# Four transformer blocks in one program: the second MLP product as three fp32r terms, and twelve score tiles a step ahead where a step has no MLP

## The chip, the cores and the metric

The kernel runs on one core of a Trainium2 chip. The metric is device time in microseconds (us) from the program's first to its last instruction; lower is better. In this text PE is the matrix engine (TensorE), PEld its weight loads, DVE the vector engine (VectorE), ACT the scalar engine (ScalarE), POOL the GpSimd engine, and SP the queue that issues most DMAs (SyncE). A line such as L1179 is a line of the kernel before; where the change is shown, the line numbers are those of the changed file.

## What is computed

Eight sequences of 256 tokens, 256 wide, go through four transformer blocks. Each block normalises, modulates by a vector made from the conditioning input, runs attention with 16 heads of width 16, and adds the result back. Blocks 0, 1 and 3 then do the same with an MLP of width 1024; block 2 has a modulated norm in its place. Block 1's attention is causal. All is float32.

```python
# blocks 0, 1 and 3 (block 1 with a causal mask); sh, sc, gt come from cond @ W_ada + b
h = layernorm(x) * (1 + sc1) + sh1
q, k, v = heads(h @ Wqkv)
x = x + gt1 * (softmax(q @ k.T / sqrt(16)) @ v @ Wo + bo)
h = layernorm(x) * (1 + sc2) + sh2
x = x + gt2 * (gelu(h @ W1 + b1) @ W2 + b2)
# block 2: scores unscaled, out-projection scaled by 1/sqrt(256),
# and after attention: x = x + gamma * layernorm(x) + beta, with no MLP
```

## The kernel before

**Steps.** The program is a chain of 32 steps, one for each pair of block (layer) and sequence: step g is layer g // 8, sequence g % 8. The order of instructions on each engine is written out by hand, and semaphores alone tie the engines together. In step g four sequences are in work: g itself is in the middle of its attention, c = g - 1 finishes (output projection, first residual, second norm, MLP), a = g + 1 gets its queries, keys and values, and n = g + 2 its first norm. A step has MLP work when c's layer has an MLP: steps 1 to 16 and 25 to 31, and sequence 31 after the last step. Steps 17 to 24 have none. The helper names used below: `q_product`, `k_product`, `v_product` (L1110, L1125), `projection` (L1139), `mlp_up` and `mlp_down` (L1165, L1179) on PE; `modulate1`, `query_hi`, `key_hi`, `value_copy`, `exps`, `gelus` on ACT; `query_lo`, `key_lo`, `ln1_a`, `ln1_c` (L777), `max_copy` (L822) on DVE.

**Exact products.** A plain fp32 product of PE runs as two recorded matmuls. The reduced form fp32r runs as one, but on rounded operands. The first MLP product `mlp_up` is therefore made of three fp32r terms: high part times high part, high times low, low times high. POOL makes the high and low parts of W1 once for each layer (`split_w1`, L474 and L476), and DVE those of the activations in each step (`ht2_split`, L908 and L910). The second product `mlp_down` is plain fp32: 16 products of a 128x128 block of `hid` and a 128x256 block of W2.

**Scores and maxima.** Queries and keys are split likewise, stored to DRAM (`spill`) and read back in an interleaved layout (`stack`: six DMAs for `q_stack`, three for `k_stack`), so that scores come from one pass. The 16 heads and two query halves make 16 score tiles of a sequence. `score` computes tile j into one of two PSUM banks and may begin when tile j - 2 has been read; DVE reads it in `maxima` (L805, or L800 where causal) and keeps the maximum of each row. The maxima of eight tiles are then split, transposed on PE (`max_turn`, L1213), copied (`max_copy`) and sent by DMA into two more rows of `q_stack` (`max_rows`, L285). `score_t` computes the scores a second time, transposed and with the maxima taken off (L1240), ACT takes the exponentials (`exps`, L613), and `values` (L1256) multiplies by V, once for heads 0 to 7 and once for 8 to 15. In step g tiles 8 to 15 of g and tiles 0 to 7 of a are made: eight tiles run one step ahead.

**The order around the change.** In an MLP step PE runs `mlp_up`, then tile 0 of a, and then the 16 products of `mlp_down` in small groups between `score_t(g, 4..7)`, tiles 1 to 7 of a and `values(g, 1)`. On POOL, `power` (L444, L446) makes the reciprocal deviations of the two norms: for c early in the step, for n once DVE has its variances. DVE's `ln1_c` waits for the latter and stands before tile 2 of a in DVE's order. In steps 17 to 24 PE begins with tiles 8 and 9, then the q and k products, then `score_t(g, 0)` and tiles 10 to 15 with the rest between them; ACT runs `query_hi` and `key_hi` before any exponential.

## Time and profile before

| what | value |
|---|---|
| median of three runs | 1170.08 us (1169.41 to 1170.24) |
| span of the profiled execution | 1170.3 us |
| PE busy | 1081.3 us, 92% |
| DVE busy | 746.0 us, 64% |
| ACT busy | 569.9 us, 49% |
| POOL busy | 174.5 us, 15% |
| mean granted clock of PE | 0.982 |

Busy time is the union of an engine's recorded instructions. PE's matmuls overlap and their ends are modelled, so how fast a stream of matmuls goes is read from their starts. An entry in brackets at the end of a timeline row is the time in which the engine stood idle before it, and what ended that.

### The profile page before, as it was taken

To read this page: it belongs to the slowest core of one execution; us is meant where nothing else is said; L and a number is where in the kernel's file an instruction comes from. 1 tells how busy PE (TensorE), PEld (TensorE's weight loads), DVE (VectorE), ACT (ScalarE), POOL (GpSimd) and SP (SyncE) were. 2 spreads that over 40 slices of the span, in tenths; PEclk is the share of its full clock that TensorE was granted. 3 is DMA by queue.
4 is the path that set the end of the run, shared out by engine and by line. 5 is a ranking of instruction groups with operands and counts; after the bars stand their busy time and mean duration, and the time that the engine had idled before them with its cause. 6 is when DMAs were issued, how large, how long until landed. Compare 5 with 4: busy or idle time off the path is not lost.

```text
span 1170.3 us, 21598 instructions
## 1 busy us (share of the span) xinstructions
PE 1081.3 (92%) x7618; PEld 858.1 (73%) x7618; DVE 746.0 (64%) x2091; ACT 569.9 (49%) x1140; POOL 174.5 (15%) x288
## 2 busy tenths in 40 slices
PE   5899999999999999999999988888888999999997
PEld 4568878788787787888787755556556877887776
DVE  4476656766567666667665666666667666676632
ACT  4254565554553445544446434444445556555452
POOL 3011110111113111101111101111114111011110
PEclk9799999999999999999999999988999999999999
DMA  7732333222345223331233433323343133321300
GB/s 236 244 115 63 102 110 109 80 65 73 110 155 186 77 78 110 110 110 60 69 102 109 137 111 102 115 94 109 110 152 128 58 100 119 119 89 66 106 4 19
DMA packets 102715, 123.21 MB, mean 105 GB/s; under 512 B 8992, under 2 KB 96032, under 8 KB 101600
## 3 DMA queue, kind: packets, MB, share of 16 engines
q1 hardware_dynamic: 102048, 121.73, 33.4%
q8 instruction: 54, 0.88, 0.3%
q10 hardware_dynamic: 576, 0.30, 0.1%
q14 instruction: 37, 0.30, 0.1%
HBM read 85.16 MB, written 35.78 MB: 103 GB/s over the span
## 4 chain that ended last, share of the span: by engine, by line
PE 71%; DVE 10%; DMA 8%; ACT 5%; issue 3%; SPq 1%; ACTq 1%; POOL 0%; DVEq 0%; POOLq 0%
PE dense L1179 13%; PE o_banks L1256 9%; PE dense L1110 9%; PE dense L1165 9%; PE s_bank L1203 8%; DMA q_stack<-max_t 7%; PE st_bank L1240 6%; PE o_banks L1139 4%; DVE neg_max L805 3%; PE o_banks L1264 3%; PE o_banks L1089 2%; ACT probs L613 2%; PE o_banks L1125 2%; PE s_bank L1213 2%; PE st_bank L1232 1%
## 5 line engine op out<-in xcount | busy, mean ns | idle before, releaser
L613 ACT ACTIVATE probs<-st_bank 128x512 f32<-128x512 f32 (+1 forms) x512 | 264.5, 570 | 172.9 <-PE st_bank L1240 121.7
L805 DVE TENSOR_REDUCE neg_max<-s_bank 128x2 f32<-128x512 f32 x384 | 256.7, 685 | 120.9 <-PE s_bank L1203 117.5
L1203 PE MATMUL s_bank<-k_stack,q_stack 96*128 96x256 f32 (+1 forms) x1024 | 233.9, 319 | 19.2 <-DMA k_stack<-qk_dram 10.1
L1203 PEld LDWEIGHTS s_bank<-k_stack,q_stack 96*128 96x128 f32 x1024 | 169.9, 194 | 61.7 <-DVE neg_max L805 20.2
L1179 PE MATMUL dense<-w_sb,hid 128*128 128x256 f32 x768 | 204.9, 381 | 0.0
L1240 PE MATMUL st_bank<-q_stack,k_stack 98*128 98x512 f32 x384 | 152.8, 471 | 15.6 <-DMA q_stack<-max_t 12.5
L444 POOL TENSOR_TENSOR veps<-mv,eps_c 128x2 f32<-128x2 f32 x65 | 13.7, 210 | 901.7 <-DVE mv L771 901.7
L1179 PEld LDWEIGHTS dense<-w_sb,hid 128*128 128x128 f32 x768 | 128.8, 189 | 9.6 <-issue 0.4
L601 ACT ACTIVATE hid<-dense,vec 128x256 f32<-128x256 f32 x192 | 80.6, 471 | 110.8 <-PE dense L1165 110.7
L1256 PE MATMUL o_banks<-probs,v_aug 128*32 128x256 f32 (+1 forms) x2048 | 124.9, 387 | 9.9 <-DVE xg L844 5.8
L1110 PE MATMUL dense<-ht,w_sb 128*128 128x256 f32 x512 | 127.2, 388 | 3.9 <-ACT ht L555 1.3
L1165 PE MATMUL dense<-ht,w_hi 128*128 128x256 f32 x384 | 116.4, 303 | 7.7 <-DVE ht_lo L910 6.5
L800 DVE CUSTOM_DVE_ANT_0 s_bank<-s_bank,mask_q 128x128 f32<-128x128 f32 (+1 forms) x256 | 86.3, 382 | 53.4 <-PE s_bank L1203 52.9
L1110 PEld LDWEIGHTS dense<-ht,w_sb 128*128 128x128 f32 x512 | 95.8, 194 | 18.0 <-issue 5.7
L1165 PE MATMUL dense<-ht_lo,w_hi 128*128 128x256 f32 x384 | 108.3, 282 | 0.0
L1165 PE MATMUL dense<-ht,w_lo 128*128 128x256 f32 x384 | 108.3, 282 | 0.0
L1256 PEld LDWEIGHTS o_banks<-probs,v_aug 128*32 128x32 f32 x2048 | 64.6, 114 | 56.2 <-issue 18.4
L1240 PEld LDWEIGHTS st_bank<-q_stack,k_stack 98*128 98x128 f32 x384 | 67.8, 190 | 44.7 <-ACT probs L613 17.5
L1165 PEld LDWEIGHTS dense<-ht,w_hi 128*128 128x128 f32 x384 | 72.9, 190 | 19.7 <-DVE ht_lo L910 10.4
L877 DVE COPY o_sb<-o_banks 128x512 f32<-128x512 f32 x46 | 31.8, 692 | 69.9 <-PE o_banks L1256 69.9
L1165 PEld LDWEIGHTS dense<-ht_lo,w_hi 128*128 128x128 f32 x384 | 73.2, 191 | 0.0
L1165 PEld LDWEIGHTS dense<-ht,w_lo 128*128 128x128 f32 x384 | 73.0, 190 | 0.0
(126 smaller groups left out, 1447.5 us busy)
## 6 DMA issues: line engine op xcount, KB each, us to landing
q_stack<-qk_dram SPq DMA_DIRECT2D x192, 128.0 KB, 2.9
k_stack<-qk_dram SPq DMA_DIRECT2D x96, 256.0 KB, 4.0
par_sb<-par_dram SPq DMA_DIRECT2D x32, 512.0 KB, 5.2
qk_dram<-q_hi SPq DMA_DIRECT2D x32, 256.0 KB, 2.1
qk_dram<-q_lo SPq DMA_DIRECT2D x32, 256.0 KB, 2.2
qk_dram<-k_hi SPq DMA_DIRECT2D x32, 256.0 KB, 2.1
qk_dram<-k_lo SPq DMA_DIRECT2D x32, 256.0 KB, 2.1
w_sb<-w SPq DMA_DIRECT2D x3, 1280.0 KB, 7.5
```

Source lines behind the costliest of these rows:

```text
L601: ins = nc.scalar.activation(hid[:, 2 * i + k], src[:, k], ACT.Gelu, bias=col(l, "b1", 2 * i + k))
L613: nc.scalar.activation(probs[p % 4][:, kt, :, q0:N], src, ACT.Exp, scale=SCORE_SCALE[l]).then_inc(p_sb, 1)
L800: ins = nc.vector.tensor_tensor_reduce(out=s, in0=s, in1=mask_q[:, (1 - qt) * P:2 * P], scale=-1.0, scalar=-MASKED, op0=ALU.add, op1=ALU.m ...
L805: nc.vector.tensor_reduce(neg_max[:, qt, 2 * p:2 * p + 2], split3(bank[:]), AX.X, ALU.max, negate=True).then_inc(s_max, 1)
L1110: ins = mm(dense[bank][:, t * N:(t + 1) * N], w_qkv(a.layer, kt, c0, c0 + P), ht1[:, kt], start=kt == 0, stop=kt == KT - 1)
L1139: ins = mm(o_bank[0][:, t * D:(t + 1) * D], ao_t[:, kt, t * P:(t + 1) * P], w_o(c.layer, kt), start=kt == 0, stop=kt == KT - 1)
L1165: ins = mm(dense[(i + 1) % 2][:, k * N:(k + 1) * N], w, h.bitcast(F32R), start=n == 0, stop=n == len(terms) - 1)
L1179: ins = mm(dense[1][:, t * D:(t + 1) * D], hid[:, j, t * P:(t + 1) * P], w_2(c.layer, j), start=j == 0, stop=j == FT - 1)
L1203: ins = mm(bank[:, e * N:e * N + k1], q_stack[g.par][0:KB, 2 * p + e, qt * P:(qt + 1) * P].bitcast(F32R), k_stack[g.par][0:KB, p, 0:k1].bi ...
L1240: mm(split3(st_bank[kt][:]), *stacks(g, p, kt, 0), start=True, stop=True).then_inc(st_ps, 1)
L1256: ins = mm(o_bank[i][32 * j:32 * j + 32, q0:N], v_aug[g.par][:, kt, 8 * h + 4 * i + j, :], pr[:, kt, j % 2, q0:N], start=kt == 0, stop=kt ...
L1264: ins = tr(o_bank[i][:, N + t * P:N + (t + 1) * P], o_sb[:, i, t * P:(t + 1) * P], ident[:])
```

## The change

It has two parts.

**The second product.** `mlp_down` becomes 48 fp32r matmuls in place of 16 fp32 ones: each product of a `hid` block and a W2 block is `hid_hi` x `w2_hi`, `hid_hi` x `w2_lo`, `hid_lo` x `w2_hi`. DVE makes `hid_hi` in four casts of 128x512 (`hidden_hi`), POOL makes `hid_lo` in four subtractions of 128x512 (`hidden_lo`), both in every MLP step. POOL splits W2 once a layer (`split_w2`, in steps 0, 9 and 25). The split of W1 moves ahead of the second norm's `power` in step 9, and from step 25 to step 24. The weights share memory in a new way: W1 of layer 1 is loaded behind the modulation weights, `q_hi` to `k_lo` lie where `hid` is, so the first GELU also waits for the spills of a; W1 has a semaphore of its own, W2 of layer 3 is loaded a step earlier, and the modulation weights of layer 3 two steps later.

**The steps without MLP work.** Steps 17 to 24 get an order of their own on PE, DVE and ACT (`attention_step`), and SP sends both halves of the maxima. Sequences 18 to 24 have twelve of their tiles made one step ahead in place of eight, so that four are left for the beginning of their own step, ahead of `q_product`.

```diff
+        w2_lo = [sb_at(f"w2_lo{i}", [P, FT, D], w_at[i] + O_2 * 4) for i in range(2)]
+        w2_hi = [sb_at(f"w2_hi{i}", [P, FT, D], w_at[1 - i] + O_1 * 4) for i in range(2)]
...
+        hid_at = xn2_at + T * D * 4
+        hid = sb("hid", [P, FT, N])
+        hid_lo = sb_at("hid_lo", [P, FT, N], hid_at)
+        hid_hi = sb("hid_hi", [P, FT, N])
+        q_hi, q_lo, k_hi, k_lo = (
+            sb_at(n, [P, KT, N], hid_at + i * KT * N * 4) for i, n in enumerate(("q_hi", "q_lo", "k_hi", "k_lo")))
...
+        def early_tiles(g):
+            return 3 * H // 4 if g.reg is None and 2 * B + 1 < g.off <= 3 * B else H // 2
...
+                if c.exists and not mlp:
+                    max_rows(sp, g, 1)
...
-                if a.exists and HAS_MLP[g.layer]:
+                if a.exists:
...
-                    load_weights(l + 1, O_O, O_2 if HAS_MLP[l + 1] else O_1, w_ld)
+                    load_weights(l + 1, O_O, O_1, w_ld)
+                    if HAS_MLP[l + 1]:
+                        load_w1(l + 1)
+                    if l + 1 == 3:
+                        load_weights(3, O_2, WCOLS, w2_ld)
...
+            def split_w2(l):
+                pool.wait_ge(w2_ld[l], 16)
+                for i in range(FT // 2):
+                    raw = w_sb[l % 2][:, O_2 + 2 * i * D:O_2 + 2 * (i + 1) * D].rearrange("p (j d) -> p j d", j=2)
+                    hi, lo = w2_hi[l % 2][:, 2 * i:2 * i + 2], w2_lo[l % 2][:, 2 * i:2 * i + 2]
+                    nc.gpsimd.tensor_copy(hi.bitcast(F32R), raw).then_inc(w2_hi_sb, 1)
+                    pool.wait_ge(w2_hi_sb, mlps_before(l) // B * FT // 2 + i + 1)
+                    nc.gpsimd.tensor_tensor(lo.bitcast(F32R), raw, hi, ALU.subtract).then_inc(w2_split, 1)
...
+            def hidden_lo(c, *chunks):
+                for i in chunks:
+                    wait(pool, hid_hi_sb, c.mlp(4, i + 1))
+                    js = slice(2 * i, 2 * i + 2)
+                    nc.gpsimd.tensor_tensor(hid_lo[:, js].bitcast(F32R), hid[:, js], hid_hi[:, js],
+                                            ALU.subtract).then_inc(hid_lo_sb, 1)
...
+                mlp = c.exists and HAS_MLP[c.layer]
                 if g.reg is None and g.off == 0:
                     split_w1(0)
+                if g.reg is None and g.off in (B + 1, 3 * B):
+                    split_w1(g.layer)
                 if c.exists:
                     power(c, 1, ln2_mv, ln2_veps, ln2_rstd)
                     if c.layer != 2:
                         pick(c, 1, mod2_now)
-                    if g.reg is None and g.off % B == 1 and g.layer > 0 and HAS_MLP[g.layer]:
-                        split_w1(g.layer)
+                if g.reg is None and g.off in (B + 1, 3 * B + 1):
+                    split_w2(g.layer)
+                if mlp:
+                    hidden_lo(c, 0, 1, 2)
                 if n.exists:
                     power(n, 0, ln1_mv, ln1_veps, ln1_rstd)
+                if mlp:
+                    hidden_lo(c, 3)
+                if n.exists:
                     wait(pool, xn1_done, n.count(1, 1))
...
-            def gelus(c):
+            def gelus(c, a):
                 l = c.layer
                 for i in range(FT // 2):
                     if i == 0:
                         wait(act, w2_ps, c.mlp(1, 0))
+                        if a.exists:
+                            wait(act, q_spill, a.count(32, 32))
+                            wait(act, k_spill, a.count(32, 32))
                     wait(act, w1_ps, c.mlp(4, i + 1))
...
+            def attention_step(g):
+                c, a = g.back(1), g.ahead(1)
+                modulate1(a)
+                if c.off > 2 * B:
+                    ao_transposed(c)
+                exps(g, 0)
+                query_hi(a)
+                exps(g, 1)
+                key_hi(a)
+                exps(g, 2, 3)
+                value_copy(a)
+                out_copy(g, 0)
+                exps(g, 4, 5, 6, 7)
+                out_copy(g, 1)
+                if g.layer > 2:
+                    ao_transposed(g)
...
+            def hidden_hi(c, *chunks):
+                for i in chunks:
+                    wait(dve, gelu_sb, c.mlp(4, i + 1))
+                    js = slice(2 * i, 2 * i + 2)
+                    nc.vector.tensor_copy(hid_hi[:, js].bitcast(F32R), hid[:, js]).then_inc(hid_hi_sb, 1)
...
+            def attention_step(g):
+                c, a, n = g.back(1), g.ahead(1), g.ahead(2)
+                modulated = modulation_of(g)
+                first, early = early_tiles(g), early_tiles(a)
+                maxima(g, *range(first, H))
+                max_split(g, 1)
+                max_copy(g, 1)
+                query_lo(a)
+                key_lo(a)
+                first_residual(c)
+                wait(dve, x1_done, c.count(1, 1))
+                norm_stats(x1, 1, ln2_stats)
+                wait(dve, ln2_stats, c.count(1, 1))
+                norm_mv(1, ln2_mv)
+                second_norm(c)
+                ln1_a(n)
+                wait(dve, ln1_stats, n.count(1, 1))
+                norm_mv(0, ln1_mv)
+                out_norm(g, 0)
+                ln1_c(n)
+                maxima(a, 0, 1, 2)
+                second_residual(c)
+                maxima(a, 3, 4, 5, 6, 7)
+                max_split(a, 0)
+                if modulated:
+                    modulation_cols(modulated)
+                out_norm(g, 1)
+                max_copy(a, 0)
+                maxima(a, *range(H // 2, early))
+                if modulated:
+                    modulation_rows(modulated)
             def step(g):
...
+                    hidden_hi(c, 0, 1)
                     if n.exists:
                         ln1_a(n)
                         wait(dve, ln1_stats, n.count(1, 1))
+                    hidden_hi(c, 2)
...
+                    hidden_hi(c, 3)
...
             def mlp_down(c, lo, hi):
+                l = c.layer
                 for i in range(lo, hi):
                     t, j = i // FT, i % FT
                     if i == 0:
-                        pe.wait_ge(w2_ld[c.layer], 16)
                         wait(pe, gelu_sb, c.mlp(4, 3))
-                    if i == 6:
-                        wait(pe, gelu_sb, c.mlp(4, 4))
-                    ins = mm(dense[1][:, t * D:(t + 1) * D], hid[:, j, t * P:(t + 1) * P], w_2(c.layer, j),
-                             start=j == 0, stop=j == FT - 1)
+                    if t == 0 and j % 2 == 0:
+                        pe.wait_ge(w2_split, (mlps_before(l) // B) * FT // 2 + j // 2 + 1)
+                        wait(pe, hid_lo_sb, c.mlp(4, j // 2 + 1))
+                    terms = ((hid_hi, w2_hi), (hid_hi, w2_lo), (hid_lo, w2_hi))
+                    for n, (h, w) in enumerate(terms):
+                        ins = mm(dense[1][:, t * D:(t + 1) * D], h[:, j, t * P:(t + 1) * P].bitcast(F32R),
+                                 w[l % 2][:, j].bitcast(F32R), start=j == 0 and n == 0,
+                                 stop=j == FT - 1 and n == len(terms) - 1)
                     if i == T * FT - 1:
                         ins.then_inc(w2_ps, 1)
...
+            def attention_step(g):
+                c, a, n = g.back(1), g.ahead(1), g.ahead(2)
+                modulated = modulation_of(g)
+                first, early = early_tiles(g), early_tiles(a)
+                def modulation_part(part):
+                    if modulated:
+                        modulation_cols(modulated, part=part, parts=4)
+                score(g, *range(first, H))
+                q_product(a, 0)
+                max_turn(g, 1)
+                q_product(a, 1)
+                score_t(g, 0)
+                k_product(a)
+                score_t(g, 1)
+                v_product(a, 0)
+                score_t(g, 2)
+                v_product(a, 1)
+                score_t(g, 3)
+                projection(c, 0)
+                projection(c, 1)
+                if modulated:
+                    wait(pe, q_lo_sb, a.count(1, 1))
+                modulation_part(0)
+                values(g, 0)
+                modulation_part(1)
+                score_t(g, 4)
+                out_turn(g, 0)
+                score_t(g, 5)
+                score(a, 0, 1)
+                score_t(g, 6)
+                score(a, 2)
+                modulation_part(2)
+                score_t(g, 7)
+                score(a, 3, 4)
+                modulation_part(3)
+                values(g, 1)
+                score(a, 5, 6)
+                out_turn(g, 1)
+                score(a, 7)
+                max_turn(a, 0)
+                score(a, *range(H // 2, early - 1))
+                ht1_t(n)
+                ao_turn(g)
+                score(a, *range(max(H // 2, early - 1), early))
+                if modulated:
+                    modulation_rows(modulated)
```

How the order stands now is shown at three places, first on PE in a step without MLP, around the beginning of the step (L1203 and L1340 score tiles, two matmuls each; L1213 and L1350 the transposed maxima; L1110 and L1243 q and k products; L1240 and L1377 `score_t`). Before:

```order
L1213 MATMUL s_bank<-ident,max_parts 16x128 x2
L1203 MATMUL s_bank<-k_stack,q_stack 128x256 x4
L1110 MATMUL dense<-ht,w_sb 128x256 x8
L1240 MATMUL st_bank<-q_stack,k_stack 128x512 x2
L1203 MATMUL s_bank<-k_stack,q_stack 128x256 x4
L1125 MATMUL o_banks<-w_sb,ht 128x256 x2
L1240 MATMUL st_bank<-q_stack,k_stack 128x512 x2
```

And now:

```order
L1350 MATMUL s_bank<-ident,max_parts 16x128 x2
L1340 MATMUL s_bank<-k_stack,q_stack 128x256 x6
L1222 MATMUL o_banks<-ident,xn 128x128 x4
L1222 MATMUL o_banks<-ident,ao 128x128 x4
L1340 MATMUL s_bank<-k_stack,q_stack 128x256 x10
L1243 MATMUL dense<-ht,w_sb 128x256 x2
L1350 MATMUL s_bank<-ident,max_parts 16x128 x2
L1243 MATMUL dense<-ht,w_sb 128x256 x2
L1377 MATMUL st_bank<-q_stack,k_stack 128x512 x2
L1243 MATMUL dense<-ht,w_sb 128x256 x4
L1377 MATMUL st_bank<-q_stack,k_stack 128x512 x2
```

Tiles 8 to 15 now stand in a row before the first q product, where two tiles stood, and no tile stands between it and `score_t(g, 5)`.

Second, ACT at the same place, from the end of one step into the next (L555 and L619 `modulate1`; L584 and L648 `ao_transposed`; L285 the DMA of the maxima; L529 and L593 `query_hi` and `key_hi`; L613 and L680 exponentials). Before:

```order
L571 ACTIVATE o_sb<-o_banks 128x512
L584 ACTIVATE ao_t<-o_banks,bv_scaled 128x256 x2
L555 ACTIVATE ht<-o_banks,mod_now 128x256 x2
L285 DMA q_stack<-max_t 1x8x256 x2
L529 ACTIVATE q_hi<-dense,vec 128x256 x2
L529 ACTIVATE k_hi<-dense,vec 128x256 x2
L613 ACTIVATE probs<-st_bank 128x512 x8
```

And now:

```order
L635 ACTIVATE o_sb<-o_banks 128x512
L619 ACTIVATE ht<-o_banks,mod_now 128x256 x2
L648 ACTIVATE ao_t<-o_banks,bv_scaled 128x256 x2
L680 ACTIVATE probs<-st_bank 128x512 x2
L593 ACTIVATE q_hi<-dense,vec 128x256 x2
L680 ACTIVATE probs<-st_bank 128x512 x2
L593 ACTIVATE k_hi<-dense,vec 128x256 x2
L680 ACTIVATE probs<-st_bank 128x512 x4
```

The high parts of queries and keys each stand behind a pair of exponentials.

Third, POOL in an MLP step (L462 and L499 the pick of a modulation; L444 with L446, and L481 with L483, `power`; L455 and L492 the addends of the residuals). Before:

```order
L462 COPY mod_now<-mod 128x4
L444 TENSOR_TENSOR veps<-mv,eps_c 128x2
L446 TENSOR_TENSOR rstd<-veps,half_c 128x2
L455 TENSOR_TENSOR xg<-xg,par_sb 128x512
L455 TENSOR_TENSOR xg<-x_sb,par_sb 128x512
```

And now:

```order
L499 COPY mod_now<-mod 128x4
L529 TENSOR_TENSOR hid_lo<-hid,hid_hi 128x512 x3
L481 TENSOR_TENSOR veps<-mv,eps_c 128x2
L483 TENSOR_TENSOR rstd<-veps,half_c 128x2
L529 TENSOR_TENSOR hid_lo<-hid,hid_hi 128x512
L492 TENSOR_TENSOR xg<-xg,par_sb 128x512
L492 TENSOR_TENSOR xg<-x_sb,par_sb 128x512
```

Three subtractions stand ahead of the `power` of n, and one between it and the addends.

## Rows read from the trace of the kernel before

**Rows 1.** The page: engines' busy time, and the chain that ended last.

```profile
PE 1081.3 (92%) x7618; PEld 858.1 (73%) x7618; DVE 746.0 (64%) x2091; ACT 569.9 (49%) x1140; POOL 174.5 (15%) x288
PE 71%; DVE 10%; DMA 8%; ACT 5%; issue 3%; SPq 1%; ACTq 1%; POOL 0%; DVEq 0%; POOLq 0%
```

**Rows 2.** Busy time by stretch: bounds, length, engines in the order of the page, clock, DMA.

```profile
198.00:233.00 35.00, 34.91 (x250) 28.66 (x250) 23.50 (x55) 19.55 (x40) 4.62 (x8) 1.00 0.31 92
764.00:795.00 31.00, 26.92 (x165) 18.53 (x164) 19.63 (x48) 13.51 (x27) 4.47 (x7) 0.89 0.32 103
833.55:862.61 29.06, 24.10 (x165) 17.18 (x165) 19.78 (x48) 13.69 (x27) 4.51 (x7) 1.00 0.50 155
```

**Rows 3.** Timeline after the last step (start, us, engine, line): both MLP products.

```profile
1152.43 0.28 PE L1165 MATMUL dense<-ht_lo,w_hi 128*128 128x256 f32 x1
...
1153.97 0.28 PE L1165 MATMUL dense<-ht,w_lo 128*128 128x256 f32 x1
...
1159.14 7.07 PE L1179 MATMUL dense<-w_sb,hid 128*128 128x256 f32 x32
1159.34 0.84 ACT L601 ACTIVATE hid<-dense,vec 128x256 f32<-128x256 f32 x2 [0.60 <-PE dense L1165]
```

**Rows 4.** Timeline of step 4 (layer 0), from the second GELU to tile 4.

```profile
199.78 0.84 ACT L601 ACTIVATE hid<-dense,vec 128x256 f32<-128x256 f32 x2 [1.27 <-PE dense L1165]
200.09 0.41 DVE L822 COPY max_t<-s_bank 16x256 f32<-16x256 f32 x1
...
201.43 0.84 ACT L601 ACTIVATE hid<-dense,vec 128x256 f32<-128x256 f32 x2 [0.81 <-PE dense L1165]
...
202.87 0.84 ACT L601 ACTIVATE hid<-dense,vec 128x256 f32<-128x256 f32 x2 [0.60 <-PE dense L1165]
...
204.31 0.69 POOL L446 TENSOR_TENSOR rstd<-veps,half_c 128x2 f32<-128x2 f32 x1
...
205.28 0.73 DVE L777 TENSOR_SCALAR xn<-x_sb,mv,rstd 128x256 f32 x2
...
208.15 0.40 PE L1203 MATMUL s_bank<-k_stack,q_stack 96*128 96x256 f32 x2
```

**Rows 5.** Lines L908, L777 and L476: durations in ns, min/median/max.

```profile
L908 DVE CAST ht<-xn x24: 426/427/891, 84.0 to 1151.0; 128x512 fp32r<-128x512 f32 x24
...
L777 DVE TENSOR_SCALAR xn<-xg,mv,rstd x48: 402/410/1433, 80.8 to 1148.7; 128x256 f32<-128x256 f32 x48
...
L476 POOL TENSOR_TENSOR w_lo<-w_sb,w_hi x12: 1262/1272/1330, 22.6 to 904.4; 128x512 fp32r<-128x512 f32 x12
```

**Rows 6.** Timeline of step 7 (causal tiles): maxima copied, and tile 4.

```profile
304.98 0.41 DVE L822 COPY max_t<-s_bank 16x256 f32<-16x256 f32 x1
...
314.22 0.34 PE L1203 MATMUL s_bank<-k_stack,q_stack 96*128 96x128 f32 x2
```

**Rows 7.** Timeline of step 23 (no MLP), q product to the next one.

```profile
833.55 3.69 PE L1110 MATMUL dense<-ht,w_sb 128*128 128x256 f32 x16
...
838.72 0.98 PE L1240 MATMUL st_bank<-q_stack,k_stack 98*128 98x512 f32 x2
839.07 2.56 DVE L805 TENSOR_REDUCE neg_max<-s_bank 128x2 f32<-128x512 f32 x4
839.18 0.36 SPq L331 DMA_DIRECT2D qk_dram<-k_lo  x1
839.32 1.08 ACT L613 ACTIVATE probs<-st_bank 128x512 f32<-128x512 f32 x2 [0.17 <-PE st_bank L1240]
...
843.47 1.91 SPq L348 DMA_DIRECT2D k_stack<-qk_dram  x3
...
850.39 0.72 PE L1203 MATMUL s_bank<-k_stack,q_stack 96*128 96x256 f32 x4
```

**Rows 8.** Issues by DMA in 820 to 865 us: KB each, median us to landing.

```profile
k_stack<-qk_dram SPq DMA_DIRECT2D x3, 256.0 KB, 4.2
```

**Rows 9.** Timeline of step 9: `power` of the second norm, before the split of W1.

```profile
367.92 0.20 POOL L444 TENSOR_TENSOR veps<-mv,eps_c 128x2 f32<-128x2 f32 x1 [18.35 <-DVE mv L771]
```

## What the change is expected to do

> **What bounds the kernel now.** I read the page first. PE is busy 92% of the span and makes up 71% of the chain that ended last, DVE 10%, DMA 8% [rows 1]. That is a mean over two kinds of step, so I took one window of each. In an MLP step PE has work in 34.91 of 35.00 us while DVE has 23.50 and POOL 4.62; such a step is bound by PE. A step without MLP has 24.10 of 29.06 us on PE and 19.78 on DVE: nobody is full, and the step is as long as its waits make it [rows 2]. So work taken off PE should pay in full in the MLP steps, unless something new makes PE wait, and a new order in the other steps must be judged by its chain, not by its work. The profiled span, 1170.3, and the median, 1170.08, are as good as one number; I sum against the span.
>
> **Part 1, what it takes off PE.** After the last step both products run with little between them. The 32 records of the fp32 product take 7.07 us from first start to last end; less the drain of the last (0.38) that is 0.216 us each, 0.432 us for a product of two. In the fp32r stream 13 steps from start to start take 1153.97 - 1152.43 = 1.54 us, so 0.1185 each and 0.355 for three terms [rows 3]. One product saves 0.077 us, an MLP 1.2 us, 24 MLPs 29 us. That is the most this part can give. Had the three terms gone no faster than the two fp32 records, the gain would be nil; nothing in the rows suggests it, since `mlp_up` already has this shape.
>
> **Part 1, what it adds.** Four casts on DVE (0.43 us each, L908 is the same form) and four subtractions on POOL (1.27 each, L476 is the same form) [rows 5]. DVE has 11 us to spare in the window and POOL 30. But products 0 and 1 now need the first cast and subtraction, products 6 and 7 the fourth, and the `power` of n stands behind three subtractions. I lay them into step 4 by its rows [rows 4]. The second to fourth GELU end at 200.62, 202.27 and 203.71; DVE is free for the first cast when `max_copy` ends, at 200.50. Two casts follow each other until 201.4.
>
> DVE's casts and POOL's subtractions also hinder each other, as the split of W1 shows: the cast L908 takes 427 ns as a rule and up to 891, the normalisation L777 410 and up to 1433, while L476 on POOL stays between 1262 and 1330 [rows 5]. I therefore let one of the two run at a time where their operands are in SBUF. Then: subtraction 1 from 201.4 to 202.65; cast 3 behind it to 203.1; subtraction 2 to 204.35; cast 4 to 204.8; subtraction 3 to 206.05; `power` (0.2 and 0.7 us) to 207.05; subtraction 4 to 208.35. In the kernel before the deviation was there at 205.00 [rows 4].
>
> The Trainium skill states the same as an exclusive lock on a shared port pair held for the whole instruction (SBUF — State Buffer, the part on engine contention). By that a cast that comes just too late takes 1.27 + 0.43 = 1.70 us, where the longest in the trace is 0.89; with every cast and normalisation at that worst the sum would be some 1 us more for each MLP step. I go by the rows.
>
> What waits: `ln1_c` (L777) began at 205.28; POOL goes on to subtraction 4 at once, so I put it behind that, 208.35 to 209.1. Tile 2 of a is reduced right after it, to 209.8, and PE's tile 4, which needs tile 2 read, starts at 209.85 in place of 208.15 [rows 4]. Products 0 to 6 have saved 0.5 us by then, all of it lost in this wait, with 1.7 us more; the nine products behind give 0.7 back. Step 4 becomes 1.0 us longer. The products 6 and 7 wait for subtraction 4 in the same stretch, which adds nothing. In layer 3 the stretch before tile 4 is about half a microsecond longer already, since `score_t(g, 4)` waits for the maxima there; I take 0.8 as the mean of the 14 steps with non-causal tiles ahead (1 to 6, 15, 16, 25 to 30). In the causal ones (7 to 14) the same layout from `max_copy` at 304.98 brings tile 4 to 314.65 where it was at 314.22 [rows 6]: the tiles start later in them, for a wait on the stacks, and the gap is smaller. With 0.7 given back behind it that is -0.2 us. Sum: 14 x 0.8 - 8 x 0.2 = +9.6. After the last step the fourth GELU ends at 1160.18 [rows 3]; casts and subtractions in turn (1.7 us a chunk, from the first GELU on) end at 1163.2, products 6 to 15 take 3.6 us, and with the drain of the last the end is at 1167.0 in place of 1166.2: +0.8. If POOL and DVE did not hinder each other, `power` would be done at 205.8, tile 4 would start at 207.95, and such a step would win 0.9 us: that is the other bound.
>
> **Part 1, the edges.** Two casts and subtractions for a quarter of W2 take 4 x (0.61 + 1.27 + 0.08) = 7.9 us a layer on POOL. In step 9 the split of W1 stands ahead of `power`; it can begin when layer 0's last product is done (some 361.5), so it ends at 369.4 where `power` began at 367.92 [rows 9]: +1.5. In step 0 the split of W2 holds the pick for `modulate1` until about when ACT needs it: +0.5. The new GELU wait on the spills has long been met. Edges: +2.
>
> **Part 2, the first half of a step.** Zero is the start of the q product; the old step has it at 833.55 [rows 7]. Old: `k_lo` is ready for its spill at 5.63 (839.18), the last of three `k_stack` DMAs is issued at 843.47 + 1.27, at 11.2, and lands 4.2 us on [rows 8], at 15.4. Tile 0 of a is issued at 16.84 and did not wait for it. New: half a q product (0.86); `max_turn` waits until 1.6, for tiles 14 and 15 at 0.64 each [rows 7] and the split; the other half to 2.6; `score_t` 0 to 3.05; k product (8 records) to 4.8; then `score_t` 1, because ACT has an exponential pair in front of `key_hi`. Its first exponential comes 0.60 after its start (838.72 to 839.32) and the pair takes 1.08 [rows 7]: 6.5. `key_hi` to 7.35, `key_lo` and the spill at 8.3, which is 2.65 later than now. SP's nine DMAs behind it are the same: landed at 18.05. PE itself would be there at 15.5 (its wait for the maxima ahead of `score_t` 4 is gone, those for the first residual and for ACT's exponentials stay). So the stacks, which cost nothing now, become the last to arrive, and tile 0 waits 2.5 us.
>
> **Part 2, the second half.** Old: 850.39 to 862.61, 12.2 us, with ten tiles. New: sixteen tiles, and DVE reads one in 0.64 to 0.66, with `second_residual`, a split, `out_norm` and `max_copy` between, of the same lengths as now: tile 4 is issued 2.7 after tile 0, `values(g, 1)` at 3.6, tile 7 at 6.75, `max_turn` 8.45, tile 9 at 9.6 behind `max_copy`, tile 11 at 11.5, tiles 13, 14 and 15 each behind DVE, the next q product at 14.3. A step takes 18.05 + 14.3 = 32.4 us against 29.06. Over steps 17 to 24: first halves 8 x 1.2 = +9.7; seven second halves 7 x 2.1 = +14.7; step 17, which has eight tiles to do ahead of its q product in place of two, +4.7; step 24, which makes only eight early, -1.5. Sum +27.6. Were the stacks in time (15.5 in place of 18.05), it would be 20.4 less, +7.2: that is the lower bound.
>
> **Sum.** 1170.3 + 9.6 + 0.8 + 2 + 27.6 = 1210.3.
>
> **Rivals.** B: engines hinder each other less, or DVE wins the race for `ln1_c`, and MLP steps win 0.9 us (22 of them and the end: -20.3), part 2 as worked out: 1179.6. For it: L908's median is undisturbed. Against: the long casts are those that met the split of W1.
>
> C: MLP steps as worked out, but the stacks come in time, by `key_hi` or the DMAs being faster than I laid them: 1170.3 + 10.4 + 2 + 7.2 = 1189.9.
>
> D, the other side: both, so that PE's saving reaches the span: 1170.3 - 20.3 + 2 + 7.2 = 1159. It holds if `power` of n is done within about 0.6 us of where it was, from where tile 4 no longer waits, and if tile 0 of a waits for no stack. Since part 2 alone is never below +7 by my chain, faster needs both, or a first half of under 14.6 us.
>
> E: more idle time on PE brings its clock down. Steps 20 and 21 show it: a window of 31.00 us has a granted clock of 0.89, the one of 29.06 us has 1.00 [rows 2], with the same instructions. If all eight steps pay these 1.9 us, it is 1210 + 15 = 1225. The Trainium skill has it that idleness sends TensorE back to the lower of its two levels (TensorE: Matmul & The Clock Gate, the part on what is happening), and the trace agrees in that the clock is 1.00 in the fullest window.
>
> **Chances and range.** A (1210) 0.42, B 0.15, C 0.15, D 0.15, E 0.13. The range leaves out D and most of what lies beyond E: 1168 to 1228. Two tenths of a percent, 2.3 us, is about what a measurement can tell from no change. Faster by more: D and a little of B and C, 0.18; within it 0.03; slower 0.79.
>
> **What would show it.** Right: in MLP steps PE waits at tile 4 of a for DVE, the casts of `hid_hi` have a mean well above 0.43 us, L777's successor a mean well above 0.41, and the second product is some 5.7 us of starts. In steps 18 to 23 tile 0 waits about 2.5 us for `k_stack`, and the step takes 32 us. Wrong: no such wait, or steps of 29 us; then the order of ACT was not what decided. If PE's stream of products does not go at 0.12 us a term, the first line of the sum falls.

## The result: 1220.7 us, 4.2% slower

| | before | after |
|---|---|---|
| median of four runs | 1170.16 us (1169.41 to 1173.03) | 1220.71 us (1218.59 to 1224.57) |
| profiled span | 1170.3 us | 1222.8 us |
| mean granted clock of PE | 0.982 | 0.941 |

The ratio is 1.0424, with a 95% interval of 1.0379 to 1.0469. The profiled execution is the slowest of the four, so the two traces lie 52.5 us apart where the medians lie 50.5. The page of the kernel after, its busy times and its chain by engine, against [rows 1]:

```profile
PE 1107.2 (91%) x8002; PEld 897.4 (73%) x8002; DVE 840.0 (69%) x2187; ACT 567.2 (46%) x1140; POOL 328.1 (27%) x408
...
PE 57%; DVE 13%; DMA 8%; issue 7%; SPq 6%; ACT 4%; POOL 3%; DVEq 0%; POOLq 0%; ACTq 0%
```

PE is busy for 26 us more although its second MLP product got cheaper, and its share of the chain fell from 71% to 57%. The first place to look is where the time sits. I took the start of each step's q product in both traces. Steps 0 to 16 together are 2.9 us longer, steps 17 to 24 are 51.6 us longer, the rest is 2 us shorter. So nearly all of the loss is in the steps without MLP work. The windows of the kernel after (length, then busy PE, PEld, DVE, ACT and POOL, then the granted clock), one MLP step, two single steps and all of steps 17 to 24, against [rows 2]:

```profile
221.90:257.20 35.30, 34.80 (x267) 29.02 (x266) 27.26 (x59) 19.52 (x39) 9.96 (x12) 1.00 0.29 90
694.80:734.60 39.80, 31.88 (x166) 22.56 (x165) 20.77 (x48) 13.37 (x27) 5.09 (x7) 0.73 0.27 81
808.00:842.30 34.30, 27.16 (x167) 18.78 (x166) 21.01 (x48) 13.37 (x27) 5.10 (x7) 0.90 0.30 94
...
651.16:947.60 296.44, 241.96 (x1352) 170.78 (x1351) 165.78 (x383) 107.05 (x216) 46.99 (x64) 0.82 0.30 95
```

Before, the same eight steps:

```profile
648.34:893.16 244.82, 208.66 (x1362) 147.09 (x1363) 160.67 (x388) 109.70 (x216) 37.22 (x56) 0.96 0.37 114
```

These two rows split the 51.6 us. PE's idle time rose from 36.2 to 54.5 us, +18.3. Its busy time rose by 33.3 us on the same number of matmuls, with the granted clock down from 0.96 to 0.82. The clock alone accounts for it: 208.7 us of work at 0.96 would be 244 at 0.82 (an estimate from the two rows), and 242 is there.

Step 21 of the kernel after, on PE, SP and ACT, where [rows 7] has step 23 before. The q product starts at 808.02; L1243 is the q and k products, L1377 `score_t`, L1340 a score tile, L1350 `max_turn`:

```profile
809.45 0.39 PE L1350 MATMUL s_bank<-ident,max_parts 128*16 128x128 f32 x2 [0.41 <-DVE max_parts L904]
...
822.21 0.98 PE L1377 MATMUL st_bank<-q_stack,k_stack 98*128 98x512 f32 x2
826.42 1.22 PE L1340 MATMUL s_bank<-k_stack,q_stack 96*128 96x256 f32 x4 [3.22 <-DMA k_stack<-qk_dram]
...
836.64 0.39 PE L1350 MATMUL s_bank<-ident,max_parts 128*16 128x128 f32 x2 [1.27 <-DVE max_parts L904]
...
840.65 1.10 PE L1340 MATMUL s_bank<-k_stack,q_stack 96*128 96x256 f32 x4 [0.55 <-DVE neg_max L892]
...
842.28 1.03 PE L1243 MATMUL dense<-ht,w_sb 128*128 128x256 f32 x4
...
810.32 1.30 SPq L307 DMA_DIRECT2D q_stack<-max_t  x2
812.88 0.37 SPq L357 DMA_DIRECT2D qk_dram<-q_hi  x1
...
816.00 0.36 SPq L357 DMA_DIRECT2D qk_dram<-k_lo  x1
...
820.29 2.79 SPq L374 DMA_DIRECT2D k_stack<-qk_dram  x3
...
813.18 1.09 ACT L680 ACTIVATE probs<-st_bank 128x512 f32<-128x512 f32 x2 [0.32 <-PE st_bank L1377]
814.15 0.84 ACT L593 ACTIVATE k_hi<-dense,vec 128x256 fp32r<-128x256 f32 x2
```

The cast of k comes behind an exponential pair, k_lo is spilled 8.0 us after the start of the q product (5.6 before), and tile 0 of a comes at +18.4, after waiting 3.2 us for the K stack (`k_stack`). That is the picture of the prediction. From tile 0 to the next q product it takes 15.9 us.

### The profile page after: what moved, and what is told of

It reads as the page before. It is cut to its first block, busy times and chain, and to the rows that moved or that the text cites. A ratio compares the mean times of both kernels' runs of the same rounds, so it can differ in the third digit from the quotient of the medians.

```text
span 1222.8 us, 22726 instructions
## 1 busy us (share of the span) xinstructions
PE 1107.2 (91%) x8002; PEld 897.4 (73%) x8002; DVE 840.0 (69%) x2187; ACT 567.2 (46%) x1140; POOL 328.1 (27%) x408
## 4 chain that ended last, share of the span: by engine, by line
PE 57%; DVE 13%; DMA 8%; issue 7%; SPq 6%; ACT 4%; POOL 3%; DVEq 0%; POOLq 0%; ACTq 0%
PE s_bank L1340 8%; PE o_banks L1393 8%; PE dense L1315 8%; PE dense L1243 8%; PE dense L1298 6%; PE st_bank L1377 5%; DMA k_stack<-qk_dram 4%; DVE neg_max L892 4%; SPq L371 4%; PE o_banks L1272 4%; DMA q_stack<-max_t 3%; PE o_banks L1222 3%; POOL hid_lo L529 2%; SPq L374 1%; PE s_bank L1350 1%
## 5 line engine op out<-in xcount | busy, mean ns | idle before, releaser
L680 ACT ACTIVATE probs<-st_bank 128x512 f32<-128x512 f32 (+1 forms) x512 | 264.6, 571 | 216.8 <-PE st_bank L1377 162.5
L1340 PE MATMUL s_bank<-k_stack,q_stack 96*128 96x256 f32 (+1 forms) x1024 | 241.5, 332 | 50.7 <-DMA k_stack<-qk_dram 35.6
L1340 PEld LDWEIGHTS s_bank<-k_stack,q_stack 96*128 96x128 f32 x1024 | 180.3, 211 | 94.1 <-DMA k_stack<-qk_dram 39.8
L529 POOL TENSOR_TENSOR hid_lo<-hid,hid_hi 128x512 fp32r<-128x512 f32 x96 | 125.8, 1320 | 267.2 <-DVE hid_hi L1004 267.2
L1377 PE MATMUL st_bank<-q_stack,k_stack 98*128 98x512 f32 x384 | 157.9, 483 | 6.6 <-DMA q_stack<-max_t 5.9
L481 POOL TENSOR_TENSOR veps<-mv,eps_c 128x2 f32<-128x2 f32 x65 | 17.9, 276 | 518.6 <-DVE mv L858 518.6
L1243 PE MATMUL dense<-ht,w_sb 128*128 128x256 f32 x512 | 135.8, 402 | 1.3 <-ACT ht L619 1.3
L1393 PE MATMUL o_banks<-probs,v_aug 128*32 128x256 f32 (+1 forms) x2048 | 131.0, 401 | 6.5 <-issue 5.8
L1315 PE MATMUL dense<-w_hi,hid_hi 128*128 128x256 f32 x384 | 115.5, 301 | 4.7 <-POOL hid_lo L529 4.6
L1243 PEld LDWEIGHTS dense<-ht,w_sb 128*128 128x128 f32 x512 | 100.0, 204 | 15.5 <-issue 1.7
L1315 PE MATMUL dense<-w_lo,hid_hi 128*128 128x256 f32 x384 | 108.8, 283 | 0.0
L1315 PE MATMUL dense<-w_hi,hid_lo 128*128 128x256 f32 x384 | 108.3, 282 | 0.0
L1377 PEld LDWEIGHTS st_bank<-q_stack,k_stack 98*128 98x128 f32 x384 | 71.3, 201 | 35.8 <-ACT probs L680 19.0
L887 DVE CUSTOM_DVE_ANT_0 s_bank<-s_bank,mask_q 128x128 f32<-128x128 f32 (+1 forms) x256 | 85.6, 383 | 16.1 <-PE s_bank L1340 15.3
L1298 PEld LDWEIGHTS dense<-ht,w_hi 128*128 128x128 f32 x384 | 72.9, 190 | 19.8 <-DVE ht_lo L997 10.5
L1004 DVE CAST hid_hi<-hid 128x512 fp32r<-128x512 f32 x96 | 73.8, 787 | 19.2 <-ACT hid L668 19.1
```

Source lines behind the costliest of these rows:

```text
L529: nc.gpsimd.tensor_tensor(hid_lo[:, js].bitcast(F32R), hid[:, js], hid_hi[:, js], ALU.subtract).then_inc(hid_lo_sb, 1)
L680: nc.scalar.activation(probs[p % 4][:, kt, :, q0:N], src, ACT.Exp, scale=SCORE_SCALE[l]).then_inc(p_sb, 1)
L887: ins = nc.vector.tensor_tensor_reduce(out=s, in0=s, in1=mask_q[:, (1 - qt) * P:2 * P], scale=-1.0, scalar=-MASKED, op0=ALU.add, op1=ALU.m ...
L1004: nc.vector.tensor_copy(hid_hi[:, js].bitcast(F32R), hid[:, js]).then_inc(hid_hi_sb, 1)
L1243: ins = mm(dense[bank][:, t * N:(t + 1) * N], w_qkv(a.layer, kt, c0, c0 + P), ht1[:, kt], start=kt == 0, stop=kt == KT - 1)
L1298: ins = mm(dense[(i + 1) % 2][:, k * N:(k + 1) * N], w, h.bitcast(F32R), start=n == 0, stop=n == len(terms) - 1)
```

## The experiments

The runs below were made together with new runs of the kernel before, which lay between 1166 and 1185 us there; so each is given as a ratio to it, with its 95% interval. The row of the kernel after keeps the ratio of its own measurement. To read the steps without MLP I cut each at tile 0 of a: the **first stretch** runs from the q product to it, the **second stretch** from it to the next q product. Means of steps 18 to 24, each from one trace, and the granted clock over steps 17 to 24:

| kernel | first | second | step | clock | ratio |
|---|---|---|---|---|---|
| before | 16.6 | 13.4 | 30.0 | 0.96 | 1 |
| after | 19.1 | 17.0 | 36.1 | 0.82 | 1.0424 |
| casts ahead | 17.8 | 16.0 | 33.7 | 0.90 | 1.0321 |
| wait filled | 19.3 | 15.4 | 34.7 | 0.89 | 1.0404 |
| eight tiles | 20.0 | 18.1 | 38.2 | 0.78 | 1.0563 |
| product first | 25.1 | 13.8 | 38.9 | 0.81 | 1.0716 |
| tiles beside | 26.4 | 15.5 | 41.9 | 0.77 | 1.0762 |

**Each part alone.** Part 1 alone takes the early return into `attention_step` away on three engines, and SP's part of it:

```diff
-            return 3 * H // 4 if g.reg is None and 2 * B + 1 < g.off <= 3 * B else H // 2
+            return H // 2
-                if c.exists and not HAS_MLP[c.layer]:
-                    attention_step(g)
-                    return
```

> Part 1 alone: the second MLP product as three fp32r terms, with the order and the eight early tiles of the kernel before in the steps without MLP work. In the trace of the changed kernel steps 0 to 16 together took only 2.9 us more than before, and steps 25 to 31 1.9 us less, so the theory that the parts are independent gives 1170.2 + 1.0 = 1171 us (1168 to 1174). The prediction's terms for the MLP work (+9.6, +0.8 and +2) give 1182.6. If the two parts hinder each other (buffers that start at one address, another semaphore for the maxima), part 1 alone is well below before: each step's second product starts and ends 1.2 us earlier, 24 x 1.2 = 29 us, 1141.

Measured 0.9973 (0.9940 to 1.0006): no difference that can be told, as the traces of the two kernels had it. Part 2 alone is the kernel before with `attention_step`, `early_tiles` and SP's order.

> Part 2 alone: the kernel before with the new order of the eight steps 17 to 24, twelve early tiles, and the maxima's rows issued by SP. If the parts are independent the whole loss of steps 17 to 24 is here: 1170.2 + 51.5 = 1222 us (1216 to 1227). By the prediction's terms for part 2 it is 1197.8. If the loss needs part 1 (a clock that is lower because of more fp32r work before), it is under 1190.

Measured 1.0525 (1.0458 to 1.0592). The whole loss is in part 2. It is even larger than in the full change, whose interval just touches this one, and above my 1222. Its trace puts 7.1 us more than the full change into the same eight steps (303.5 against 296.4, at a clock of 0.81); whether part 1 takes that off, or the executions differ, I leave open.

**Casts ahead.** ACT's casts and PE's k product again ahead of the exponentials and of `score_t`, as in the kernel before; the rest of the change kept:

```diff
-                exps(g, 0)
                 query_hi(a)
-                exps(g, 1)
                 key_hi(a)
-                exps(g, 2, 3)
+                exps(g, 0, 1, 2, 3)
...
                 q_product(a, 1)
-                score_t(g, 0)
                 k_product(a)
+                score_t(g, 0)
```

> The changed kernel with the products and casts of Q and K taken ahead again in the eight steps: TensorE makes the K product straight behind the Q product, ahead of the first pair of transposed scores, and ScalarE casts query and key ahead of its exponentials, as the kernel before did. Theory A (the stacks of the next step are asked for too late, since ScalarE casts between exponentials): the wait of the first early score tile for the K stack (3.2 us in step 21, 22.8 us over seven steps) falls under 1 us each, SP's spill of k_lo starts some 3 us sooner behind the Q product, and the time falls by 20 to 25 us for the wait alone, to 1195 to 1200. Rival (the order of VectorE sets the steps: it is the neg_max of each tile that is late): the wait for the stack goes over to a wait for neg_max, and the time stays within 5 us of 1220.7. Rival (the clock): the waits go but the granted clock stays near 0.8, and busy time of TensorE stays at 212 us over the eight steps against 183 before.

Measured 1.0321 (1.0279 to 1.0364), some 12 us less than the change, by two ratios of different measurements whose intervals lie 0.15% apart. PE's longest waits over steps 17 to 24 in the kernel after (total us, times, longest):

```profile
PE s_bank L1340 <- DMA k_stack<-qk_dram: 26.1, 8, 4.7
PE s_bank L1350 <- DVE max_parts L904: 12.2, 13, 1.3
```

and in this one:

```profile
PE s_bank L1348 <- DVE max_parts L902: 12.6, 14, 1.3
PE s_bank L1338 <- DMA k_stack<-qk_dram: 8.9, 7, 2.0
PE st_bank L1375 <- ACT probs L680: 8.1, 8, 1.0
```

The mechanism holds, two thirds of the stack wait went, but half of that came back as a wait for exponentials, which now stand behind the casts. The step is still 3.7 us above the kernel before, 2.6 of it in the second stretch, whose order this edit doesn't touch. By the ratios the late casts are a quarter of the loss; in the traces steps 17 to 24 get 22.2 of their 51.6 us back. The 29.4 us that are left there are read from this trace and not tried: PE is idle for 12.2 us more than in the kernel before, with 12.6 us for the split maxima of a turn where the kernel before waits 3.3, and busy for 17.2 us more, at a clock of 0.90 in place of 0.96.

**The wait filled.** In the seven steps without modulation, 28 matmuls that nobody reads stand in the wait:

```diff
+                if not modulated:
+                    wait(pe, q_lo_sb, a.count(1, 1))
+                    for _ in range(28):
+                        mm(dense[0][:, 0:2 * P], ident_b[:], mask_k[:], start=True, stop=True)
                 score(a, 0, 1)
```

> The changed kernel with 28 matmuls whose results nobody reads (128 x 256, bf16) put ahead of the first early score tile in seven of the eight steps, where TensorE waits for the K stack. Over steps 17 to 24 the changed kernel needs 46.6 us more than before, of which 29.7 are TensorE busy for longer on the same 1190 matmuls (granted clock 0.82 against 0.95) and 16.9 are waits. Theory (the clock falls because TensorE stands still there): the granted clock of the steps rises to 0.95 or more and the time falls to 1190 to 1205. Rival (the clock has to do with other waits or with what came before): the clock stays near 0.82, and the time stays at 1221 or rises by up to 2 us a step, to 1235.

Measured 1.0404 (1.0362 to 1.0446), not to be told from the change. The trace tells more than the ratio. Steps 17 to 24 in its windows:

```profile
655.80:943.42 287.62, 248.77 (x1548) 179.33 (x1547) 167.23 (x383) 107.06 (x216) 45.81 (x64) 0.89 0.32 98
```

and the wait for the stack in them:

```profile
PE s_bank L1340 <- DMA k_stack<-qk_dram: 5.6, 5, 2.5
```

Most of the stack wait is filled (26.1 us to 5.6) and the clock rises from 0.82 to 0.89, so standing still there does lower it. Steps 18 to 24 are 1.4 us shorter on average, all of it in the second stretch (17.0 to 15.4). The first stretch, which ends when the stack lands, is no shorter (19.1 and 19.3). Steps 17 to 24 together are 8.8 us shorter and the whole trace is 5.0 shorter; a gain of that size is at the edge of what the ratio can show. So the clock is a cost on top of the waits: half of its fall was worth 1.4 us a step in this one trace, where my rival E had 1.9.

**Eight tiles.** `early_tiles` returns 8 again, in the full change.

> The changed kernel with eight instead of twelve early score tiles in the eight steps 17 to 24; all else of both parts stays. Theory of the loop (a period is the time from the Q product to the landed stacks, 18.4 us in step 21, and behind it, in a row, sixteen score tiles with their maxima, since the Q product of the next step stands behind the last of the tiles whatever their split; 15.9 us): the time stays, 1214 to 1228, and tile 0 still waits 2 to 5 us for the K stack. Rival (the four tiles that were taken ahead lengthen the step on VectorE, four times 0.65 us each step): 2.6 us x 7 = 18 us less, 1202.

Measured 1.0563 (1.0490 to 1.0636): both expectations were wrong. Twelve early tiles are better than eight in this order. Comparing step 21 of the change with step 22 of this run: from `max_turn(a, 0)` to the next q product it is 5.6 us with twelve tiles and 7.7 with eight. With twelve, the two groups of transposes at the step's end lie between tiles, beside DVE's maxima; with eight nothing is left to do beside them. This is argued from rows, not tried.

**Product first.** With the casts ahead, PE's q and k products also ahead of tiles 12 to 15, and DVE's subtractions ahead of their maxima.

```diff
-                score(g, *range(first, H))
                 q_product(a, 0)
-                max_turn(g, 1)
                 q_product(a, 1)
+                k_product(a)
+                score(g, *range(first, H))
+                max_turn(g, 1)
```

> The changed kernel with the casts ahead (as in the run before it) and, in the eight steps, TensorE's Q and K products also ahead of the last score tiles 12 to 15 and the turn of the maxima, VectorE's subtractions ahead of those tiles' maxima. Theory of the loop: the remaining tiles (about 4 x 0.9 us) then lie beside the way of the stacks and not ahead of it, and the steps fall from 33.8 us to 30 to 31 us, 8 x 3 = 24 us below the 1211.3 measured with the casts ahead: 1185 to 1192. Rival (VectorE or the maxima's rows set the steps): the transposed score tile 4 waits longer for the maxima's rows instead and the time stays at 1205 to 1215.

Measured 1.0716 (1.0636 to 1.0796). The second stretch did what the theory of the loop said, 16.0 to 13.8. The first grew from 17.8 to 25.1. SP's timeline (q product at 815.84) has a part of the reason:

```profile
826.69 1.30 SPq L307 DMA_DIRECT2D q_stack<-max_t  x2
828.04 0.44 SPq L357 DMA_DIRECT2D qk_dram<-q_hi  x1
...
829.57 0.50 SPq L357 DMA_DIRECT2D qk_dram<-k_lo  x1
```

The maxima's rows of g stand ahead of the spill in SP's order, and SP waits for them: `q_hi` is cast by 819.9 and spilled 8 us later. I had moved work on PE and DVE and not looked at the queue behind which the spill stands. But PE is late as well:

```profile
820.33 0.83 PE L1338 MATMUL s_bank<-k_stack,q_stack 96*128 96x256 f32 x4
823.25 1.10 PE L1338 MATMUL s_bank<-k_stack,q_stack 96*128 96x256 f32 x4 [2.09 <-DVE neg_max L890]
825.62 0.60 PE L1348 MATMUL s_bank<-ident,max_parts 128*16 128x128 f32 x2 [1.27 <-DVE max_parts L902]
...
841.88 1.09 PE L1338 MATMUL s_bank<-k_stack,q_stack 96*128 96x256 f32 x4 [2.29 <-DMA k_stack<-qk_dram]
```

It is ready for tile 0 at 839.6, already 23.8 us behind the q product, and then waits 2.3 us for the stack; over steps 17 to 24 that wait is 10.9 us, hardly more than the 8.9 with the casts ahead. The larger part of the growth is tiles 12 to 15 and their turn, which now stand in the first stretch with their waits (5.5 us from 820.33), and the lower clock (0.81 against 0.90).

**Tiles beside.** Twelve early tiles with the kernel before's order of the first half: tiles 12 to 15 between `score_t(g, 0)` and `score_t(g, 2)`. It uses the later terms and split of part 1 described below.

> The better part 1 with a part 2 mended by the readings so far: twelve early tiles stay, but the last tiles 12 to 15 stand behind the Q and K products, between the transposed scores, as in the kernel before (first pair of transposed scores ahead of them), with casts and subtractions of Q and K ahead. In the changed kernel a step is the time from Q product to the first early tile (19.1 us) and from there over all sixteen tiles to the next Q product (17.0 us); in the kernel before it is 16.6 + 13.4 with ten tiles in the second stretch. Theory of the loop: the first stretch is the stacks' own 17.5 us, the second has twelve tiles, 14 to 14.7 us: steps of 31.5 to 32.2 us, 7 x 2 us above part 1's 1164, 1174 to 1181, far below 1220. Rival (it is the twelve early tiles as such, on VectorE and on SP's queue): steps stay at 34 to 36 us, 1195 to 1210. Second rival (with the tiles beside the stacks the early ones are pure gain): below 1164.

Measured 1.0762 (1.0676 to 1.0848). Here SP's order is the reason (q product at 821.28; the last row is from the waits of steps 17 to 24):

```profile
832.81 1.30 SPq L307 DMA_DIRECT2D q_stack<-max_t  x2
834.15 0.44 SPq L357 DMA_DIRECT2D qk_dram<-q_hi  x1
...
847.52 1.22 PE L1343 MATMUL s_bank<-k_stack,q_stack 96*128 96x256 f32 x4 [8.91 <-DMA k_stack<-qk_dram]
...
PE s_bank L1343 <- DMA k_stack<-qk_dram: 74.2, 8, 10.8
```

PE is ready for tile 0 at 838.6, 17.3 us behind the q product, and the stack comes 8.9 us later. In the kernel before, ACT sent these rows in such steps, and SP spilled `q_hi` at +2.9. In the change they are SP's, ahead of the spill; this fits `max_turn` standing inside the q product there, with all sixteen tiles in a row. Whether twelve tiles pay with the rows on another queue stayed untried.

**Where part 1's saving goes.** First the terms with `hid_lo` two chunks of j later in the first half of `mlp_down`, on top of part 1 alone:

```diff
-                    terms = ((hid_hi, w2_hi), (hid_hi, w2_lo), (hid_lo, w2_hi))
+            for j in range(FT + 2):
+                if j < FT:
+                    DOWN += [(j, 0, w2_hi), (j, 0, w2_lo)]
+                if j >= 2:
+                    DOWN.append((j - 2, 1, w2_hi))
```

> Part 1 alone, with the terms of hid_lo taken two chunks of j later in the first half of the second product (the products with hid_hi run ahead). In an MLP step of part 1 alone TensorE waits 0.49 us at the first term with hid_lo and 0.46 us at the one of the last chunk, while the step is 35.2 us as before. Theory (TensorE's waits for POOL's hid_lo eat the saving): 0.5 to 0.9 us a step less in the 22 MLP steps, 1148 to 1157 where part 1 alone measured 0.9973 of before (1167). Rival (something else sets the step: the maxima's rows for the transposed score tile 4, or VectorE with its four casts): within 4 us of 1167.

Measured 0.9976 (0.9943 to 1.0010). PE's waits for `hid_lo` are gone from the trace (1.7 us in steps 1 to 16 without the edit) and steps 1 to 7 still take 35.16 us on average, against 35.20 in part 1 alone and 35.65 before, where one step of 37.6 raises the mean. Then POOL's split of layer 0's W2 in step 1 in place of step 0:

> The kernel with the later hid_lo terms, and POOL's split of the first layer's W2 moved from the end of step 0 into step 1, behind the copy of the scale and shift that step 1's Q product waits for. In part 1 alone step 0 is 41.2 us against 36.6 before, with that copy 8.5 us later on POOL. Theory (the copy behind the split costs the 4.6 us, and they are not given back): 4 to 5 us below the run with the later terms. Rival (what step 0 loses is given back later, or step 1 now waits for w2_split): within 1.5 us of it.

Measured 0.9949 (0.9913 to 0.9985). POOL copies the scale and shift for step 1's q product at 66.75, where part 1 alone has:

```profile
75.57 0.18 POOL L497 COPY mod_now<-mod 128x4 f32<-128x4 f32 x1
```

Step 0 falls from 41.2 to 38.2 us, and step 1 takes 2 us of it back (35.2 to 37.3). The fall is no clean measure of the split: PE's idle time in step 0 went from 4.5 to 3.9 us only, the rest is busy time at a clock of 0.84 in place of 0.78, and the run without table loads below, which has the same late split, takes 40.7 us at 0.78. The ratio is 0.3% lower with intervals that overlap. Among the versions that keep every part of the product it is the only one whose interval lies below the kernel before, by 0.5% in the middle.

Next, VectorE's casts in the first MLP step alone. Later steps then take their high part from that old one: `hid_lo` makes up the difference, with coarser rounding.

> Part 1 with the later hid_lo terms and the later split, and VectorE's four casts of hid_hi made in the first step with MLP work only: the later steps multiply with the hid_hi of that step (the product is then not the reference's). It frees VectorE of 3.2 us a step, the drawn-out casts of 1.5 us beside POOL among them. Every MLP step there takes 35.1 to 35.3 us whether transposed tile 4 comes 18.7 or 20.4 us behind the Q product. Theory (ScalarE is the floor: last Gelu, table load of 1.28 us, exponentials 4 to 7): the steps stay at 35.0 to 35.2, within 3 us of 1164 (0.9949 of before). Rival (VectorE's maxima of the early tiles behind the casts are the floor, neg_max waits of 0.45 us at tile 3): 0.5 to 0.9 us a step less, 1145 to 1153.

Measured 0.9922 (0.9885 to 0.9960). Then ACT's table loads away, in part 1 and in the kernel before:

> Part 1 with the later hid_lo terms and the later split, and the Gelu replaced by the identity, with both table loads of an MLP step left out (the product is then not the reference's). Theory (ScalarE's way from the last Gelu over the table load to the exponentials 4 to 7 is the floor under the step): the MLP steps fall from 35.2 to about 34.0 to 34.3 us, the whole by 20 to 25 us against 1164, to 1140 to 1145, and this kernel is 15 to 25 us below its twin without the three-term product. Rival (the floor is VectorE, or the maxima's rows): under 5 us less than 1164.

> The kernel before with the same edit: Gelu replaced by the identity, no table loads (the product is then not the reference's). If TensorE itself sets the MLP steps of the kernel before (34.98 of 35.20 us busy in step 5), nothing is won: 1165 to 1171, steps of 35.0 to 35.2. If ScalarE's way is the floor there too, it falls by 10 to 25 us as well, and part 1 then still wins nothing against it.

Measured 0.9924 (0.9881 to 0.9968) and 0.9970 (0.9931 to 1.0010). The run without casts fits ScalarE as the floor, but the one without table loads refutes it: no floor was lifted by 1 us. In none of the three does an MLP step that is non-causal throughout (1 to 6, 25 to 29) go below 34.9 us. Their timelines say why. With the casts gone, PE waits at the turn of the maxima:

```profile
234.85 1.28 POOL L528 TENSOR_TENSOR hid_lo<-hid,hid_hi 128x512 fp32r<-128x512 f32 x1 [9.11 <-ACT hid L665]
234.97 1.19 DVE L896 CAST max_parts<-neg_max 128x16 fp32r<-128x16 f32 x1
...
236.50 0.38 PE L1350 MATMUL s_bank<-ident,max_parts 128*16 128x128 f32 x2 [0.50 <-DVE max_parts L898]
```

This run doesn't relieve VectorE cleanly: POOL no longer waits for the casts, its first subtraction falls beside VectorE's split of the maxima, and that small cast takes 1.19 us in place of 0.17.

With the table loads gone, it waits at tile 3 of a, for DVE and its casts:

```profile
247.86 0.50 PE L1334 MATMUL s_bank<-k_stack,q_stack 96*128 96x256 f32 x2 [0.86 <-DVE neg_max L883]
```

Cut at `score_t(g, 4)`, the rest of an MLP step takes 16.0 to 16.4 us in the kernel before whenever it comes. In the kernel after it takes 15.3 to 15.4 when `score_t(g, 4)` comes 19.8 us behind the q product or later (steps 2, 26 to 29), 15.7 at 19.4 (step 4) and 16.4 to 16.5 when it comes by 18.8 (steps 3, 5, 6), with step 1 between (19.0, 16.2); step 25 alone doesn't fit (20.9, 16.3), and has W2's split in it. Step 1 is the same (20.9, 16.4) in the run that moves the split there. PE's own saving of 0.8 us is there, but only in steps where PE comes late to `score_t(g, 4)`. When PE is early it meets ScalarE and VectorE, which are no earlier than before. As I read it, two or three chains end within a few tenths of each other, and taking one away shows the next; taking two away at once wasn't tried. The clock takes a part as well: step 9 has a granted clock of 0.92 to 0.96 in all eleven traces with part 1, and 1.00 in the three without.

## Why the prediction came out as it did

**Direction and range** held: slower, 1220.7 in 1168 to 1228. The point, 1210, missed by 10.7 us. Against the trace (1222.8) it missed by 12.5, through errors that partly cancel: -15.4 for the MLP steps, +5.4 for the edges, +24.0 for part 2 and -1.5 for the end, where I had +0.8. That the point came so close is luck.

**Part 1's price for PE** held: each of the three terms takes 0.12 us from start to start, 0.36 in all, against 0.43 for an fp32 product of two records.

**MLP steps, +9.6: too high.** Steps 1 to 7, 9 to 16 and 25 to 29 came out 5.8 us shorter together. The step that failed is the layout of VectorE and POOL, and with it the wait of PE at tile 4. In step 4 I had tile 4 of a 7.2 us behind tile 0; it came after 5.9 (5.5 before):

```profile
202.30 0.74 DVE L1004 CAST hid_hi<-hid 128x512 fp32r<-128x512 f32 x2
...
204.26 1.47 DVE L1004 CAST hid_hi<-hid 128x512 fp32r<-128x512 f32 x1 [0.56 <-ACT hid L668]
...
208.30 1.61 DVE L864 TENSOR_SCALAR xn<-x_sb,mv,rstd 128x256 f32 x2 [0.33 <-POOL rstd L483]
...
202.78 2.66 POOL L529 TENSOR_TENSOR hid_lo<-hid,hid_hi 128x512 fp32r<-128x512 f32 x2 [11.53 <-DVE hid_hi L1004]
...
208.15 1.28 POOL L529 TENSOR_TENSOR hid_lo<-hid,hid_hi 128x512 fp32r<-128x512 f32 x1
...
210.56 0.50 PE L1340 MATMUL s_bank<-k_stack,q_stack 96*128 96x256 f32 x2
```

The hindrance is real: the cast at 204.26 takes 1.47 us, up to the end of the second subtraction at 205.44 and 0.3 more, and the 96 casts have a median of 428 ns and a mean of 787. But I had let the second subtraction wait for cast 3, and it did not: POOL's two ran back to back. That brought everything behind it forward by about 0.9 us. Then `ln1_c` did not stand behind subtraction 4 but beside it, 1.61 us long, which gives the other 0.3. PE doesn't wait at tile 4 at all, and over steps 1 to 7 it waits 0.2 us for DVE's maxima at a score tile: the sign that I had named is missing. The Trainium skill says that, for the VectorE forms that use it, whichever of the two engines starts first holds the shared port pair and the other blocks (SBUF — State Buffer, the part on two separate sides); this trace agrees, and in these rows it is mostly VectorE that pays.

**Edges, +2: too low.** The traces have +4.9 for step 0 and +2.5 for step 8. I had the copy for `modulate1` of step 1 arriving "about when ACT needs it", +0.5. It came 8.7 us later than before, at 75.77, but `ht` was done at 77.06 and the q product starts at 81.23, so PE did not wait for it. What differs is the clock. The stretch from 60 to 70 us in the kernel after, in the kernel before, and in the kernel before without table loads, which is the same program there since step 0 has no MLP:

```profile
60.00:70.00 10.00, 10.00 (x59) 7.59 (x61) 6.14 (x15) 3.78 (x8) 3.85 (x5) 0.56 0.01 4
60.00:70.00 10.00, 8.68 (x74) 6.03 (x74) 7.58 (x23) 3.89 (x8) 2.29 (x4) 1.00 0.01 2
60.00:70.00 10.00, 10.00 (x60) 7.27 (x59) 5.54 (x13) 3.26 (x6) 2.29 (x4) 0.52 0.01 2
```

Step 0 takes 41.5, 36.6 and 40.6 us in these three, so most of the +4.9 is a clock that also comes without the change. What the split of W2 costs PE there is a longer wait for DVE's split maxima, 2.7 us against 2.0, and 4.2 in three other traces with the split in step 0.

In step 8 PE waits 3.2 us for DVE's maxima (0.5 before). I had priced the moved split of W1 by what stands behind it on POOL. It begins at 359.8, still in step 8, and VectorE works beside it:

```profile
360.53 1.27 POOL L512 TENSOR_TENSOR w_lo<-ada_sb,w_hi 128x512 fp32r<-128x512 f32 x1
360.62 1.74 DVE L931 TENSOR_TENSOR x_sb<-prod,xg 128x512 f32<-128x512 f32 x1
361.75 1.07 POOL L510 CAST w_hi<-ada_sb 128x512 fp32r<-128x512 f32 x1
...
363.00 1.45 DVE L833 TENSOR_TENSOR row_out<-prod,row_in 8x256 f32<-8x256 f32 x1
...
368.10 0.44 PE L1340 MATMUL s_bank<-k_stack,q_stack 96*128 96x128 f32 x2 [3.19 <-DVE neg_max L887]
```

The two VectorE operations take 0.69 and 0.41 us in the kernel before, and five of them together lose 3.4 us ahead of the maxima that PE waits for. It is the hindrance that I had in the MLP steps and left out here.

**Part 2, +27.6: 51.6.** The mechanism is A's: tile 0 waits for the stack, 3.2 us in step 21 against 2.5, k_lo is spilled at 8.0 against 8.3. The first stretch was 18.4 in that step against 18.05, the second 15.9 against 14.3, and the means over steps 18 to 24 are 19.1 and 17.0. The failing step is that I used durations at full clock in steps that I expected to be idle for longer: my +27.6 is idle time throughout, and the trace has 18.3 us more idle and 33.3 more busy. I had the clock as rival E, as an alternative with a chance of its own, where it follows from A: longer waits, lower clock, longer work. A with E was 1225, and with the MLP steps as measured (15.4 less) 1210; 33.3 us of longer busy time against E's 15 is the largest error of size. And ACT's order, which I took for what decides, was worth a quarter of the loss by the ratios when it was put back; the larger rest lies in waits for the maxima and in the clock.

## What to carry to other kernels

When an order is changed so that a step waits more, cost its work at the clock that rows with as much idle time show, not at the full one; here the two came together. Before a producer is moved, look what stands ahead of its consumer on the DMA queue: in the run with tiles beside, SP's wait for the maxima cost PE 74 us of waiting for the stack. Before a longer step is put down to the change, compare its granted clock with other traces of the same program, as step 0 shows. And where an engine is 99% busy, taking work off it can give next to nothing: here two others end close behind it.

## What the runs showed of the hardware

Filling a 3 us wait with unread matmuls raised the granted clock of eight steps from 0.82 to 0.89 and left the time of the whole where it was, within what the ratio can show. The hindrance between VectorE and POOL weighed mostly on VectorE: the same cast of 128x512 took between 0.39 and 1.57 us, POOL's subtraction between 1.26 and 1.55. POOL pays too: its own cast of 128x512, 0.61 us as a rule, took 1.07 beside VectorE in step 8. And the same instructions had a granted clock of 1.00 in one execution and 0.52 in another over the same 10 us of step 0, which made that step 4 us longer.
